# Last expert sum accumulated into the residual rows by GpSimd transfers, with a changed order of statistics, sends and shared-expert units

## What is computed

```python
x = x + tanh(g_xattn) * xattn(ctx, ctx, layernorm(x), ssm_kernel, D, 8)
x = x + tanh(g_ffn) * ffn(layernorm(x), w_norm, w_router, w_gate, w_up, w_down, sw_gate, sw_up, sw_down, w_shared_gate)
# xattn: per head outer products k*v, a causal long convolution with the head's kernel, product with q
# ffn: rms norm, router over 32 experts, the 4 best of a token; an expert takes at most 128 token slots;
#   y = (silu(buf @ w_gate) * (buf @ w_up)) @ w_down, weighted and summed back to the tokens
#   + sigmoid(x @ w_shared_gate) * ((silu(x @ sw_gate) * (x @ sw_up)) @ sw_down)
```

## Time and profile before

| what | us |
|---|---|
| median of 3 runs | 332.99 (330.82 to 333.48) |
| the profiled execution | 335.25 |
| its span, first to last instruction | 333.5 |
| TensorE busy | 300.6 (90%) |
| VectorE busy | 214.5 (64%) |
| GpSimd busy | 200.1 (60%) |
| ScalarE busy | 123.9 (37%) |

### The profile page before, as it was taken

The page is one execution under the profiler, slowest core; times in us unless marked ns, Lnnn a source line. Parts: engine busy times, 40 slices in busy tenths (PEclk is TensorE's granted clock), DMA queues, the critical chain, the costliest instruction groups (busy, mean ns, idle before and its releaser), DMA issues.

```text
span 333.5 us, 5037 instructions
## 1 busy us (share of the span) xinstructions
PE 300.6 (90%) x1548; PEld 249.6 (75%) x1548; DVE 214.5 (64%) x518; ACT 123.9 (37%) x352; POOL 200.1 (60%) x233
## 2 busy tenths in 40 slices
PE   5899868965999989999699999499999999998993
PEld 4798768954998778998478777277777777876782
DVE  2689996764859997679854711034454454368696
ACT  3248344952277401449026801134334334231000
POOL 3998996437688957784476777116665663342300
PEclk9999988997999999999899999789999999999998
DMA  5997999995011111021077730519999999977287
GB/s 186 291 316 221 292 268 385 386 279 174 36 71 47 62 53 53 36 68 38 18 204 227 227 87 1 142 58 227 218 249 226 251 233 235 301 179 238 31 267 239
DMA packets 52970, 59.40 MB, mean 178 GB/s; under 512 B 6570, under 2 KB 48550, under 8 KB 52944
## 3 DMA queue, kind: packets, MB, share of 16 engines
q1 hardware_dynamic: 42272, 47.24, 47.2%
q0 software_dynamic: 7392, 8.69, 13.3%
q10 hardware_dynamic: 3280, 3.15, 2.9%
HBM read 36.83 MB, written 26.94 MB: 191 GB/s over the span
## 4 chain that ended last, share of the span: by engine, by line
PE 52%; DVE 16%; SPq 13%; DMA 7%; issue 5%; POOL 5%; DVEq 0%; ACT 0%
PE Y L1268 12%; PE pg L1101 6%; POOL dispatched L415 5%; PE pu L1101 5%; SPq L322 4%; PE pd L1287 4%; PE Y L1287 4%; SPq L312 4%; SPq L318 3%; PE Y L1089 3%; PE Y L1090 3%; PE Y L1091 3%; DVE arena L802 3%; PE Y L1259 3%; DMA arena<-in_ctx_dram 2%
## 5 line engine op out<-in xcount | busy, mean ns | idle before, releaser
L415 POOL DMA_INDIRECT dispatched<-rows,dsu x64 | 64.0, 1000 | 32.0 <-issue 24.6
L494 POOL DMA_INDIRECT expert_sum<-arena,ide x30 | 47.6, 1588 | 57.0 <-DVE arena L984 31.2
L405 POOL TENSOR_TENSOR arena<-arena 128x256 f32<-128x256 f32 x96 | 57.4, 634 | 4.0 <-ACT arena L508 3.6
L970 DVE TENSOR_TENSOR arena<-arena,Y 128x176 f32<-128x176 f32 x32 | 10.8, 337 | 47.5 <-ACT arena L708 42.6
L1089 PE MATMUL Y<-arena 128*128 128x192 f32 x128 | 33.9, 348 | 5.9 <-DVE arena L794 5.3
L802 DVE TENSOR_REDUCE arena<-arena 128x128 f32<-128x1024 f32 x32 | 38.7, 1211 | 0.2
L1091 PE MATMUL Y<-arena 128*128 128x192 f32 x128 | 33.1, 342 | 0.0
L1090 PE MATMUL Y<-arena 128*128 128x192 f32 x128 | 33.1, 342 | 0.0
L701 ACT ACTIVATE arena<-Y,wn 128x128 f32<-128x128 f32 x64 | 20.0, 363 | 33.6 <-PE Y L1259 33.4
L1089 PEld LDWEIGHTS Y<-arena 128*128 128x128 f32 x128 | 22.9, 201 | 9.9 <-issue 7.2
L1268 PE MATMUL Y<-arena 128*128 128x352 f32 x88 | 29.7, 460 | 0.0
(11 more groups left out here) (215 smaller groups left out, 670.9 us busy)
## 6 DMA issues: line engine op xcount, KB each, us to landing
expert_sum<-zrow SPq DMA_DIRECT2D x3, 2176.0 KB, 17.5
dispatched<-zrow SPq DMA_DIRECT2D x1, 4624.0 KB, 21.7
arena<-dispatched SPq DMA_DIRECT2D x32, 144.5 KB, 3.8
arena<-in_L_ffn_w_gate_dram SPq DMA_DIRECT2D x22, 176.0 KB, 2.8
arena<-in_L_ffn_w_up_dram SPq DMA_DIRECT2D x22, 176.0 KB, 3.9
arena<-in_L_ffn_w_down_dram SPq DMA_DIRECT2D x22, 176.0 KB
first_slots<-expert_sum SPq DMA_DIRECT2D x4, 512.0 KB, 6.2
arena_sum<-expert_sum SPq DMA_DIRECT2D x4, 512.0 KB, 6.3
```

Of the source, the lines that this page charges most:

```text
L405: ins = pool.tensor_tensor(o[:, :, blk], i0, i1, ALU.mult)
L415: pool.indirect_dma_start(buf, bass.IndirectOffsetOnAxis(ap=dsu[:, t % 2, j:j + 1], axis=0), rows[:, t % 2, j // K, :], None, bounds_check ...
L494: pool.indirect_dma_start(accs[a], bass.IndirectOffsetOnAxis(ap=ide[:, e % NO:e % NO + 1], axis=0), ye[:, e % NO, :], None, compute_op=ALU ...
```

## The change

- `SOLO` 26 to 28: experts 26 and on no longer all go to sum 0; expert 27 goes to sum 1. `LOAD1_AT` 26 to 28, `ADD1_AT` 28 to 29: sum 1 is loaded in one go at expert 28 and added at experts 29 and 30.
- Unit 32 moves from behind expert 25 to ahead of the experts, with banks pg and pu. Unit 33 moves from behind expert 26 to behind expert 25; unit 34 stays behind expert 27.
- Sum 0 is no longer loaded by SyncE and added by VectorE. GpSimd issues eight transfers that accumulate the sum's rows into `x_sb`, after all adds to sum 0 have landed and VectorE has finished with sum 1.
- ScalarE's statistics of group g + 2 are cut in two (sums at p = 6, squares at p = 7; both at p = 5 before). `query_pow` of GpSimd follows the products of p = 7. One `send` of group 2 moves ahead of `xn_low` of group 3. `token_slots` is cut in two, and for group 0 the second part runs in step (2, 0).

```diff
-CLOSE, SOLO, OWN = 23, 26, 2
+CLOSE, SOLO, OWN = 23, 28, 2
-LOAD2_AT, LOAD1_AT = 23, 26
-ADD2_AT, ADD1_AT = 25, 28
+LOAD2_AT, LOAD1_AT = 23, 28
+ADD2_AT, ADD1_AT = 25, 29
-TWICE = range(20, 32)
+TWICE, LAST_BANKS = range(20, 33), 31
-UNITS_EXPERT = range(32, 40)
-UNIT_STEP = {25: (32,), 26: (33,), 27: (34,), 29: (35, 36, 37), 30: (38, 39)}
+UNITS_EXPERT = range(33, 40)
+UNIT_STEP = {25: (33,), 27: (34,), 29: (35, 36, 37), 30: (38, 39)}
...
-                if LOAD1_AT <= e < LOAD1_AT + G:
-                    load_sum(1, e - LOAD1_AT)
-            for i in range(2 * G):
-                load_sum(0, i)
+                if e == LOAD1_AT:
+                    for i in range(G):
+                        load_sum(1, i)
...
                     if p == 1:
                         token_pow(t)
-                    if p == 6 and g + 2 < G:
-                        query_pow(g + 2)
                     if p in (4, 5):
                         xn_low(t, p - 4)
                     if p == 7:
+                        if g + 2 < G:
+                            query_pow(g + 2)
                         send(t, 0)
             for i in range(1, 3):
                 send(G - 2, i)
             token_pow(G - 1)
-            for i in range(3, 5):
+            for i in range(3, 6):
                 send(G - 2, i)
             for c in range(2):
                 xn_low(G - 1, c)
 
             pool.wait_ge(s["lg_ready"], G)
-            for i in range(5, 8):
+            for i in range(6, 8):
                 send(G - 2, i)
...
+            pool.wait_ge(add_sem[0], all_added(0))
+            pool.wait_ge(s["sum1_used"], 1)
+            for i in range(2 * G):
+                if i == 2 * G - 2:
+                    pool.wait_ge(s["down_used"], GB * G)
+                rows_ = B * S // (2 * G)
+                pool.dma_start(x_sb[:, 2 * i:2 * i + 2, :], accs[0][i * rows_:(i + 1) * rows_, :].rearrange("(b p) l -> p b l", p=P),
+                               accum_op=ALU.add).then_inc(fin_sem[0][i], 16)
...
-                    if p == 7 and g + 2 < G:
-                        q_coef(g + 2)
-                        query(g + 2, 0)
...
+                    if p == 6 and g + 2 < G:
+                        q_stats(g + 2)
+                    if p == 7 and g + 2 < G:
+                        q_squares(g + 2)
+                        q_coef(g + 2)
+                        query(g + 2, 0)
...
-                        if g + 2 < G:
-                            q_stats(g + 2)
...
                     if p == 6 + (g == 1):
-                        token_slots(t)
+                        token_ranks(t)
+                        if g > 1:
+                            token_slots(t)
+                    if (g, p) == (2, 0):
+                        token_slots(0)
...
-                if e == ADD1_AT + 2:
+                if e == ADD1_AT + 1:
                     add_sum(1, G - 2)
                     add_sum(1, G - 1)
+                    dve.sem_inc(s["sum1_used"], 1)
                 for m in UNIT_STEP.get(e, ()):
                     use(m)
                     downs[0] += m % UNITS >= NJ
+                    if m == 36:
+                        add_sum(1, 0)
+                        add_sum(1, 1)
...
             def add_own(i):
                 dve.wait_ge(s["own_done"], i + 1)
-                after(two[i])
+                dve.wait_ge(fin_sem[0][i], 16)
...
             for i in range(2 * G):
-                dve.wait_ge(fin_sem[0][i], 16)
-                two[i] = mark(dve.tensor_tensor(x_pair(i), x_pair(i), sums[0][:, 2 * i:2 * i + 2], ALU.add))
-                if i:
-                    add_own(i - 1)
-            add_own(2 * G - 1)
+                add_own(i)
...
-                elif n == TWICE[-1]:
+                elif n == LAST_BANKS:
                     pe.wait_ge(s["rank_used"], G)
+                elif n > LAST_BANKS and n in TWICE:
+                    pe.wait_ge(s["down_used"], GB * gs)
```

More of the change, by code:

```diff
@@ L208, in in_y @@
         def in_y(n):
-            return n in TWICE and (NJ * (n // UNITS) + n % UNITS) % 2 == 0
+            return n in TWICE and n < LAST_BANKS and (NJ * (n // UNITS) + n % UNITS) % 2 == 0
         def gate_out(n):
-            return pd[:] if n == TWICE[-1] else Y[:, 0] if in_y(n) else pg[:]
+            return pd[:] if n == LAST_BANKS else Y[:, 0] if in_y(n) else pg[:]
         def up_out(n):
-            return pm[:] if n == TWICE[-1] else Y[:, 1] if in_y(n) else pu[:]
+            return pm[:] if n == LAST_BANKS else Y[:, 1] if in_y(n) else pu[:]
         def down_out(n):
@@ L242, in flamingo_block @@
             gate_done up_done silu_done act_ready down_done down_used dve pool
-            e_tr e_xT e_gu e_silu e_act e_atr e_aT e_y e_yout sum2_used iota_ready onehot_done y_high y_low own_done fin_add""".split()
+            e_tr e_xT e_gu e_silu e_act e_atr e_aT e_y e_yout sum1_used iota_ready onehot_done y_high y_low own_done fin_add""".split()
         s = {n: sem(n) for n in names}
@@ L345, in load_sum @@
                     sp.wait_ge(add_sem[a], all_added(a))
-                if a:
-                    sp.wait_ge(s["e_y"], (0, LOAD1_AT, LOAD2_AT)[a] + i)
+                if a == 2:
+                    sp.wait_ge(s["e_y"], LOAD2_AT + i)
                 elif i == 0:
-                    sp.wait_ge(s["sum2_used"], 1)
+                    sp.wait_ge(s["e_y"], LOAD1_AT)
                 n = FINE[a] * G
@@ L541, in q_stats, with q_squares @@
                 own(act_e.activation(nmq[:], qsum[:], ACT.Copy, scale=-1.0 / L))
+            def q_squares(g):
                 for b in range(GB):
@@ L638, in _ @@
             q_stats(2)
+            q_squares(2)
             act_e.wait_ge(s["sw_in"], 64)
@@ L897, in token_gates, with token_ranks @@
                 sgf_mark[t] = mark(dve.tensor_scalar(sgf[:, t], ez[:], tg[:, 1:2], None, ALU.mult))
-            def token_slots(t):
+            def token_ranks(t):
                 dve.wait_ge(s["rank_done"], t + 1)
@@ L904, in token_slots @@
                 dve.tensor_tensor(carry[:], carry[:], pm[:, GB * E:(GB + 1) * E], ALU.add).then_inc(s["rank_used"], 1)
+            def token_slots(t):
                 link(dve.scalar_tensor_tensor(out=rk[:], in0=ge[:], scalar=FAR, in1=rk[:], op0=ALU.mult, op1=ALU.add))
@@ L1044, in _ @@
             dve.wait_ge(s["down_used"], GB * G)
-            two = {}
             def add_own(i):
                 dve.wait_ge(s["own_done"], i + 1)
-                after(two[i])
+                dve.wait_ge(fin_sem[0][i], 16)
                 dve.tensor_tensor(x_pair(i), x_pair(i), own_out(i).rearrange("p (b l) -> p b l", b=2), ALU.add).then_inc(s["fin_add"], 1)
             for i in range(2 * G):
-                dve.wait_ge(fin_sem[0][i], 16)
-                two[i] = mark(dve.tensor_tensor(x_pair(i), x_pair(i), sums[0][:, 2 * i:2 * i + 2], ALU.add))
-                if i:
-                    add_own(i - 1)
-            add_own(2 * G - 1)
+                add_own(i)
         @block.tensor
@@ L1120, in gate @@
                     pe.wait_ge(s["silu_done"], k)
-                    if n == UNITS_EXPERT[0]:
-                        pe.wait_ge(s["down_used"], GB * gs)
                 split_product(gate_out(n), gs, j * P if j < NF else 2 * NF * P).then_inc(s["gate_done"], 1)
@@ L1127, in up @@
                 if j < NF:
-                    if n == TWICE[-1]:
+                    if n == LAST_BANKS:
                         pe.wait_ge(s["rank_used"], G)
+                    elif n > LAST_BANKS and n in TWICE:
+                        pe.wait_ge(s["down_used"], GB * gs)
                     elif n in TWICE:
@@ L1254, in x_tr @@
                 if e == 0:
-                    pe.wait_ge(s["act_ready"], NJ * (UNITS_EXPERT[0] // UNITS) + UNITS_EXPERT[0] % UNITS - 1)
+                    pe.wait_ge(s["act_ready"], NJ * (LAST_BANKS // UNITS) + LAST_BANKS % UNITS)
                 if e:
@@ L1273, in a_tr @@
                 if e == 0:
-                    pe.wait_ge(s["act_ready"], NJ * (UNITS_EXPERT[0] // UNITS) + UNITS_EXPERT[0] % UNITS)
+                    pe.wait_ge(s["act_ready"], NJ * (LAST_BANKS // UNITS) + LAST_BANKS % UNITS + 1)
                 else:
```

## The result

The changed kernel has a median of 337.81 us (336.56 to 338.17, 4 runs) against 333.24 us for the one before (330.82 to 333.65, 4 runs, with the three shown ahead). The ratio is 1.0129, with an interval of 1.0085 to 1.0173: slower by about 1.3%. The forecast of 333.5 us said no change; the range of 326.5 to 342 holds the result, and my own range for the likeliest case (330.5 to 336) does not. By the 1% that the prediction took as the mark of a change, the result is slower, a case that it gave 0.28.

The account below looks back on a forecast made before the run. The chain was held by TensorE for 52%, VectorE 16%, SyncE's queue 13%. Terms of -6.4 us up to the owned products and +6.9 in the tail gave +0.5, so 333.5 us, range 326.5 to 342.

Parts of the forecast that it names:

- the likeliest case: Whole kernel: about no change, transfer period 1.7 to 2.35 us, 330.5 to 336 us; chance 0.36, 0.30 within 1%.
- the rival at 342.7: Eight accumulating transfers of the last sum: period 3.2 us, +9.7 us, slower than before; chance 0.21.
- Early edits: Group 1 statistics, token_slots(0) and query_pow: 0 us, since TensorE waits for a context until 79.15; range -0.5 to +1.5.
- send(2, 5): Dispatch on GpSimd: two scatters moved ahead of xn_low(3) start the last 16 scatters earlier, -0.7 us (0 to -1.5).
- Unit 32: Moved into TensorE's wait before the experts: -2.75 us in the loop, -2.4 us from the clock staying up.
- Sum 1: Expert loop: later add removes TensorE's wait at unit 35, -1.3 us; waiting behind the loads costs +0.7 us.
- The last sum: Tail: eight accumulating GpSimd transfers, period p 2.05 us; 20.6 instead of 13.7 us from the owned products, +6.9.
- the first rival: Last sum's transfers cost GpSimd no more than a plain scatter: period 1.28 us, 327.4 us; chance 0.33.
- the last term: End of the tail, behind the last transfer's landing: one add and the last store, 0.68 + 2.75 us.
- Cheap transfers: Index-free transfers of the last sum at plain scatter cost, overlapped with stores: period 1.28 us, -5.6 us; chance 0.33.
- Dear transfers: Last sum's transfers limited by descriptor writing or engine time: period 3.2 us, deciding from 2.4 up, +9.7 us; chance 0.21.
- Gains fail: Ahead of the tail: clock falls despite unit 32, or sum 1's loads come later; 336.2 us, chance 0.10.

Follow-up runs that it names:

- e9: Changed kernel with the last sum as before and all edits of statistics, powers, slots and sends undone; ratio 0.9825 to the kernel before.
- e1: Changed kernel with only the last sum as before (eight SyncE loads, sixteen VectorE adds); 328.88 us, ratio 0.9804 to the kernel before.
- e8: Changed kernel with the last sum as before, run again as base for e9; ratio 0.9853 to the kernel before.
- e12: Changed kernel with the last sum as before, run again as a base on another chain's chip; ratio 0.9860 to the kernel before.
- e3: Changed kernel with ScalarE holding all eight stores until the eighth sum has been added; run once, span 335.0 us.
- e5: Kernel before with only units 32 and 33 moved as in the change; ratio 0.9936 to the kernel before.

## Why the prediction was right, and where it was off

**Direction and size.** I forecast no change, since 6.4 us gained ahead of the tail would be lost in it. The result is 1.3% slower, outside the 1% of that case. I had given 0.02 to being slower with a period between 1.7 and 2.35 us, which is what came. The measured 337.81 lies 4.3 us from the forecast and 4.9 from the rival at 342.7, so the wide range did part of the work. Both halves are there: 6.0 us gained at the first owned product, and a tail of 335.7 - 313.84 = 21.9 us instead of 13.7, 8.2 lost where I had 6.9. By the profiled spans that makes +2.2 instead of +0.5. The rest of the distance to the measured +4.6 is that the profiled execution of before was 2.0 us above its median; a forecast that carries a difference over from one execution has this in it.

**Early edits: right (0).** `e9` shows it. The transposes that wait for the last context come at 78.37 instead of 79.15, and 0.2 us is left of all early gains at the first expert, less than executions of one kernel differ by there (212.34, 212.77 and 213.84 in `e1`, `e8` and `e12`).

**send(2, 5): forecast -0.7, measured -0.2** at the first expert's transposes (212.69 for 212.91). The sends of the last group start at 189.07, not 188.6: the destinations were ready at 188.3 instead of 187.8. The step from the transposes at 164 to the destinations was slower in this execution, which had 0.50 and 0.69 of the clock there; in `e3` it was 1.00. That part wanders between executions: `e1`, `e8` and `e12`, the same kernel, had 0.83, 0.66 and 0.85 from 160 to 170 us.

**Unit 32: right.** -2.75 us of the loop and the clock. The first down product came at 218.95 instead of 221.53, 2.6 us earlier, of which 0.2 is the send's: -2.4 for the clock, as forecast. What I did not see is that the term hangs on the sum 1 edit, as `e5` and `e9` show.

**Sum 1: right in kind, its net size by luck.** I took -1.3 us for a wait that goes and +0.7 for waiting behind the loads. The wait at unit 35's product only fell from 1.37 to 0.74 us, and nothing was paid behind it: from there to the first owned product both kernels take 12.1 us. The net is -0.6, forecast and measured, and -0.2, -2.4, -2.75 and -0.6 make the 6.0 us measured. VectorE waited 1.30 and 0.35 us for loads (up to 2 forecast), and sum1_used came at 312.4, the first transfer at 312.93, against 312.0. The last add to sum 0, issued at 301.80, landed 7.1 us later, at 308.9, inside the 308 to 310.

**The last sum: the period was right, for the wrong half of its reason, which is luck.** I took p = 2.05 near the accumulating scatter's 1.85 of GpSimd. Landings were 1.99 us apart. But GpSimd does not set it: the eight issues overlap and take 9.72 us in all, the last begins at 318.0, (318.0 - 312.9) / 7 = 0.73 us behind the one before it on average. My floor of 1.28 for the issue was too high. The engines' time sets p: 1.73 for the transfer, inside my 0.8 to 2.4, and 0.80 for the store. Eight of both are 20.2 us, of the 22.8 from the first issue to the end of the span (335.7 - 312.93). The landings are closer than the sum of the two, since the stores fall behind them. The Trainium skill, "DMA: Bandwidth & Descriptors", section "Anatomy of one DMA — SWDGE (gpsimd) path", calls descriptor generation small, and the trace agrees with its 0.73 us for 256 rows; that this spoke for the first rival was my reading, and it did not follow, since the period came from the engines. From first issue to the last add it took 18.4 us against a forecast of 18.6.

**What was mis-sized** is the last term, 0.68 + 2.75 behind the last landing: from 331.36 it took 4.3 us to the end, not 3.4, since stores held up beside the transfers were still being worked off when the last was issued. With a start 0.9 us late that makes nearly all of the 1.7 us between the forecast end of 334.0 and the span of 335.7.

**Rivals.** Cheap transfers: fell, though their condition on the issue (no indices) held. Dear transfers (p from 2.4): fell on p, but right on the mechanism named for it, that an accumulate takes the engines about twice as long per KB, though less than its 2.4 us. Gains fail: fell, the clock stayed up.

## What to carry over

An accumulating transfer saves an engine's instruction and a landing buffer, but here it took the DMA engines 1.73 us for 256 KB where a plain one took 0.90, and it held up the stores of its own tail. In this tail, where the adds cost 0.6 us each and the loads were issued 6 us ahead of them, load and add were 8 us better. And a move that fills an idle stretch ahead of a stage can be worth its time nearly twice where it keeps TensorE's clock up (2.75 and 2.4 us here), if the transfers that the later stage waits for keep pace: without the changes to sum 1 the kernel gained 0.64%, with them 1.75%.

## What the hardware showed that I had not expected

- GpSimd issues direct transfers of 256 rows 0.73 us apart, less than the indirect ones of 128 rows at 1.28 and 1.85. Single instructions show as lasting up to 4.6 us, and they overlap.
- Eight plain transfers from that queue went in 640 packets for 2.10 MB, eight accumulating ones in 2176.
- A wait of 3.36 us cost TensorE another 2.7 us by the clock that it left behind (5.75 instead of 3.05 us for one unit; the granted clock was 0.50 from 304 to 308 us of `e5`).
- GpSimd and VectorE adding on-chip operands together slow each other: 1.74 and 1.18 us in the median, instead of VectorE's 0.68 alone.
